# One product that turns and adds, shorter limits, hinted loops and a zeroing in blocks, in an attention and deformable-convolution kernel

## The chip, the cores and the metric

The kernel runs on one core of a Trainium2 chip, as one program. The core has a matrix engine (PE, which multiplies a weight tile held in it by a moving tile), and three engines for elementwise work: DVE (VectorE), ACT (ScalarE) and POOL (GpSimd). SP issues transfers. They run on their own and wait for each other on semaphores. The metric is the time of one execution in microseconds (us) on the device. Before the change the median of 3 runs was 2442.1 us (2438.3 to 2442.82).

## The reference

Two layers, cut to what matters. The change touches the second one alone.

```python
# layer 0: group norm, attention over 4096 positions of each of 4 images, x + projection
# layer 1, x: (4, 128, 64, 64) f32
out = relu(batchnorm(conv2d(x, w1), g1, b1))
offsets = conv2d(out, w_off) + b_off          # 18 channels: 9 row, 9 column offsets
out = batchnorm(deform_conv(out, offsets, w2), g2, b2)
return relu(out + x)
# deform_conv: per pixel and tap, p = pixel + tap + offset, limited to the padded image,
#   four neighbours gathered and weighted by distance, then a 3x3 product with w2
```

## The kernel before, in words

Each engine has its own instruction list, written by hand as a Python function under `@block`. A helper `after(engine, key, count)` makes the engine wait for a semaphore. Nothing is reordered: an engine runs its list as written. Where a list repeats, a loop with a register (`Fori`) runs on that engine alone, and the branch back at its end needs no other engine.

Four stages follow each other.

1. Attention (up to 1552 us in the trace), written by `schedule`. Its loops are not touched by the change.
2. The first 3x3 convolution (1567 to 1695 us), in 32 blocks of 512 pixels (8 image rows). POOL prepares the input (lines 412 to 421), ACT and DVE split it into two f16 parts, PE multiplies, and DVE writes `Y` and its statistics. Each engine has a loop over the 4 images.
3. The offset stage (1699 to 1828 us), again 32 blocks. For block n ACT makes `HT`, the normalised rows (line 608). DVE makes its two f16 parts `PDh` and `PDl` (lines 950 and 952), which PE needs one block later. PE turns `HT` by four transposes (line 1190) and multiplies the offset weights by 27 small products in four column groups of 32 (line 1200), so the sum over taps and parts ends up in four parts. Two blocks later PE turns these rows so that pixels stand on partitions (line 1208, four transposes per block). ACT copies them into `OR` (line 598), still as four parts. When all 8 blocks of an image are there, DVE runs `offset_finish` (lines 922 to 940): three additions of the parts, one of the bias, two limits and one maximum, each over 128x576 values. It stands in DVE's list after block 5 of the next image, and for the last image at the end. Beside this ACT and DVE stage the turned `HT` in one of two buffers `XS` (lines 583 and 957), and SP stores each block with four transfers (line 302). ACT must wait for those of two blocks earlier. POOL zeroes `Y` image by image once ACT has read it (line 435).
4. The sampling stage (1842 to 2391 us): 128 groups of 128 pixels, in 8 half images of 16 groups. POOL builds interpolation weights (line 457), PE transposes them (line 1227), ACT and DVE split them, PE samples and multiplies `w2`. PE runs the first half image outside a loop and the other seven in `pe.Fori(1, NHALF)` at line 1270, whose body is one half image: 960 products, each with a weight load. DVE's loop also has one half image a pass, those of ACT and POOL have two.

The numbers of a block run through all engines, so a late DVE block stops PE one block later, and through the copies of line 598 ACT too.

Of the kernel before, what the change touches and what calls it, by code (L numbers as in the profile page):

```python
# [28 lines left out]
NCH = N // 512  # L29
# [38 lines left out]
V_NW, V_NB, V_BQ, V_BK, V_BV, V_BP, V_G1, V_B1, V_G2, V_B2 = range(W_VEC, W_VEC + 10)  # L68
W_BOFF = W_VEC + 10
W_A = W_BOFF + NOFF  # L70
# [15 lines left out]
K_ALL = K_CB + 6  # L86
# [4 lines left out]
FIN = 7  # L91


def build(nc, x, weights, consts, out):
# [6 lines left out]
    with ctx:  # L101
# [60 lines left out]
        OR = sb_in(l1d, "offset_parts", [128, B * 32, 4, NOFF], F32)  # L162
# [75 lines left out]
        def vec(i):  # L238
            return WF[:, i:i + 1]

# [93 lines left out]
        def _(po):  # L334
# [88 lines left out]
            with po.Fori(0, B) as b:  # L423
                for rb in range(NCH):
                    conv1_in(b, rb)
# [36 lines left out]
            with po.Fori(0, npass) as n:  # L462
# [10 lines left out]
                with po.Fori(0, NHALF // 2 - 1) as u:  # L473
                    half_image(u * 2, 0, False)
                    half_image(u * 2 + 1, 1, False)
# [7 lines left out]
        def _(act):  # L483
# [88 lines left out]
            with act.Fori(1, B) as b:  # L572
                conv1_image(b, False)
# [43 lines left out]
            with act.Fori(1, B) as b:  # L617
                offset_image(b, range(NCH), False)
# [24 lines left out]
            with act.Fori(0, npass) as n:  # L643
# [28 lines left out]
                with act.Fori(0, NHALF // 2 - 1) as u:  # L672
# [13 lines left out]
        def _(ve):  # L686
# [14 lines left out]
            boff = WF[:, W_BOFF:W_BOFF + NOFF][:, None, :].to_broadcast([128, GPI, NOFF])  # L701
# [190 lines left out]
            with ve.Fori(1, B) as b:  # L892
# [29 lines left out]
            def offset_finish(b):  # L922
# [3 lines left out]
                parts = [OR[:, bass.ds(b * GPI, GPI), g, :] for g in range(4)]  # L926
                after(ve, "ocp", b * NCH + NCH)
                ve.tensor_tensor(od, parts[0], parts[1], ALU.add).then_inc(s["fin"], 1)
                after(ve, "fin", f0 + 1)
                ve.tensor_tensor(od, od, parts[2], ALU.add).then_inc(s["fin"], 1)  # L930
                after(ve, "fin", f0 + 2)
                ve.tensor_tensor(od, od, parts[3], ALU.add).then_inc(s["fin"], 1)
                after(ve, "fin", f0 + 3)
                ve.tensor_tensor(od, od, boff, ALU.add).then_inc(s["fin"], 1)
                after(ve, "fin", f0 + 4)
                ve.tensor_tensor(od, od, low, ALU.max).then_inc(s["fin"], 1)
                after(ve, "fin", f0 + 5)
                ve.tensor_tensor(od, od, HIGH[:, :, :], ALU.min).then_inc(s["fin"], 1)
                after(ve, "fin", f0 + 6)
                ve.tensor_reduce(SM[:, bass.ds(b + 48, 1)], od, AX.XY, ALU.max, apply_absolute_value=True).then_inc(s["fin"], 1)  # L940

            def h1_split(b, rbs, first):
                for rb in rbs:
# [18 lines left out]
            with ve.Fori(1, B) as b:  # L962
                h1_split(b, range(NCH), False)
            h1_split(B - 1, range(NCH, NCH + 2), False)
            offset_finish(B - 1)
# [6 lines left out]
            l1(ve.scalar_tensor_tensor(CNT[0:1, :], CL[0:1, K_CA - K_LO:K_CB - K_LO], SM[0:1, 30:31], CL[0:1, K_CB - K_LO:K_ALL - K_LO], ALU.mult, ALU.add))  # L972
            assert lstep[0] == L1_FLAG
            after(ve, "fz", B)
# [27 lines left out]
            with ve.Fori(0, npass) as n:  # L1002
# [25 lines left out]
                with ve.Fori(1, NHALF) as h:  # L1028
# [13 lines left out]
        def _(pe):  # L1042
# [122 lines left out]
            with pe.Fori(0, B) as b:  # L1165
# [15 lines left out]
            pe.wait_ge(s_wc, 4)  # L1181
# [184 lines left out]
```

## Time and profile before

| | us |
|---|---|
| median of 3 runs | 2442.1 |
| profiled execution, its own time | 2438.34 |
| its span, first to last instruction | 2436.4 |
| PE busy | 2260.8 |
| DVE busy | 1817.6 |
| ACT busy | 1797.5 |
| POOL busy | 1438.8 |

The profile is of one execution. Its time is 1.9 us more than its span, and it lies at the low end of the three runs. The granted clock (PEclk) is the share of full speed at which PE may run; its two levels are 1.2 and 2.4 GHz, so 0.50 means the lower one. Idle time is put down to what ended it; `issue` is idle time for which the profile shows no wait.

### The profile page before, as it was taken

What the parts mean: (1) busy time and instruction counts of PE and PEld (TensorE: products, weight loads), DVE (VectorE), ACT (ScalarE), POOL (GpSimd) and SP (SyncE); (2) the same over time, 40 slices, a digit from 0 to 9 for tenths busy, and PEclk for the clock granted to TensorE, in tenths of its full rate; (3) what the DMA queues carried; (4) which work ended last, traced back from release to release, by engine and by line L of the source; (5) the groups of instructions that cost most, each with busy time, mean ns of one, the idle gap of its engine ahead of it and who ended that gap; (6) DMA issues with size and microseconds to landing.
All of it is one profiled execution on the core that took longest, in us unless ns stands there. A gap on an engine that the chain in (4) does not pass through costs nothing.

```text
span 2436.4 us, 72880 instructions
## 1 busy us (share of the span) xinstructions
PE 2260.8 (93%) x26541; PEld 1819.8 (75%) x26541; DVE 1817.6 (75%) x3901; ACT 1797.5 (74%) x2963; POOL 1438.8 (59%) x1067
## 2 busy tenths in 40 slices
PE   5999999999999999999999999698867999999992
PEld 3777777777767777777777777587437999999992
DVE  6778877778877777877777777587666877777875
ACT  5788888888888888888888888432646766666764
POOL 4668656666656666655666666662117665556650
PEclk9999999999999999999999999899988999999996
DMA  3999999999999999998998999871224433333336
GB/s 92 194 174 169 171 180 166 177 176 173 177 176 161 174 177 173 172 160 155 177 175 176 175 177 176 222 226 49 74 66 140 123 116 116 115 116 115 115 100 276
DMA packets 1048676, 378.77 MB, mean 155 GB/s; under 512 B 975344, under 2 KB 1035376, under 8 KB 1040240
## 3 DMA queue, kind: packets, MB, share of 16 engines
q1 hardware_dynamic: 1048432, 375.42, 73.6%
q8 instruction: 165, 2.70, 0.5%
q14 instruction: 79, 0.65, 0.1%
HBM read 98.76 MB, written 41.68 MB: 58 GB/s over the span
## 4 chain that ended last, share of the span: by engine, by line
PE 70%; POOL 10%; issue 8%; DVE 4%; DMA 4%; ACT 1%; SPq 1%; POOLq 0%; DVEq 0%; ACTq 0%
PE psum L1045 14%; PE psum L1046 14%; PE psum L1047 14%; POOL probs_split L365 9%; PE psum L1085 7%; PE psum L1087 6%; PE psum L1086 6%; PE psum L1227 6%; DMA probsT_dma<-probs_split 2%; PE psum L1071 2%; PE psum L1200 1%; DMA final<-x_scratch 1%; DVE neg_max L714 1%; DVE padded_hi L950 1%; DMA xt_scratch<-xt_stage 0%
## 5 line engine op out<-in xcount | busy, mean ns | idle before, releaser
L365 POOL TENSOR_TENSOR probs_split<-probs,probs_split 128x896 f16<-128x896 f32 x512 | 967.2, 1889 | 526.6 <-ACT probs_split L515 526.5
L714 DVE TENSOR_REDUCE neg_max<-psum 128x1 f32<-128x1024 f32 x512 | 626.3, 1223 | 309.1 <-PE psum L1047 306.7
L512 ACT ACTIVATE probs<-psum,exp_bias 128x1024 f32<-128x1024 f32 x512 | 570.5, 1114 | 186.0 <-DVE exp_bias L716 184.8
L1085 PE MATMUL psum<-vT_hi,probsT_dma 128*128 128x129 f16 x3584 | 637.6, 221 | 12.9 <-DMA probsT_dma<-probs_split 12.7
L1087 PE MATMUL psum<-vT_hi,probsT_dma 128*128 128x129 f16 x3584 | 637.2, 219 | 0.0
L1086 PE MATMUL psum<-vT_lo,probsT_dma 128*128 128x128 f16 x3584 | 637.0, 218 | 0.0
L515 ACT ACTIVATE probs_split<-probs 128x896 f16<-128x896 f32 x512 | 486.5, 950 | 24.1 <-DMA probsT_dma<-probs_split 1.6
L457 POOL TENSOR_TENSOR interp<-row_hats,col_hats 128x360 f32<-128x360 f32 x384 | 294.8, 797 | 208.9 <-PE psum L1227 204.0
L1045 PE MATMUL psum<-k_hi,q_hi 128*128 128x512 f16 x1024 | 388.4, 379 | 4.0 <-DVE q_lo L830 2.5
L1046 PE MATMUL psum<-k_lo,q_hi 128*128 128x512 f16 x1024 | 388.6, 379 | 0.0
L1047 PE MATMUL psum<-k_hi,q_lo 128*128 128x512 f16 x1024 | 388.6, 379 | 0.0
L1085 PEld LDWEIGHTS psum<-vT_hi,probsT_dma 128*128 128x128 f16 x3584 | 347.5, 97 | 15.9 <-DMA probsT_dma<-probs_split 15.5
L1086 PEld LDWEIGHTS psum<-vT_lo,probsT_dma 128*128 128x128 f16 x3584 | 352.8, 98 | 0.0
L1087 PEld LDWEIGHTS psum<-vT_hi,probsT_dma 128*128 128x128 f16 x3584 | 345.0, 96 | 0.0
L984 DVE TENSOR_TENSOR interpT_lo<-psum,interpT_hi 120x384 f16<-120x384 f32 x384 | 191.1, 550 | 80.9 <-ACT interpT_hi L632 80.0
L641 ACT ACTIVATE sampled_hi<-psum 128x432 f16<-128x432 f32 (+1 forms) x384 | 182.6, 496 | 88.7 <-PE psum L1047 88.4
L992 DVE TENSOR_TENSOR sampled_lo<-psum,sampled_hi 128x432 f16<-128x432 f32 (+1 forms) x384 | 207.4, 554 | 49.7 <-ACT sampled_hi L641 45.4
L632 ACT ACTIVATE interpT_hi<-psum 120x384 f16<-120x384 f32 x384 | 162.0, 491 | 83.2 <-PE psum L1227 81.4
L1045 PE MATMUL psum<-sampled_hi,weights_hi 128*128 128x128 f16 x1152 | 215.3, 221 | 0.6 <-DVE sampled_lo L992 0.6
L1047 PE MATMUL psum<-sampled_hi,weights_lo 128*128 128x128 f16 x1152 | 213.9, 220 | 0.0
L1046 PE MATMUL psum<-sampled_lo,weights_hi 128*128 128x128 f16 x1152 | 213.6, 220 | 0.0
L1045 PE MATMUL psum<-interpT_hi,xt_windows 120*128 120x144 f16 x1024 | 211.0, 229 | 0.0
(181 smaller groups left out, 4898.2 us busy)
## 6 DMA issues: line engine op xcount, KB each, us to landing
xt_windows<-xt_scratch SPq DMA_DIRECT2D x192, 320.0 KB
xt_scratch<-zeros_f SPq DMA_DIRECT2D x28, 576.0 KB, 4.3
probsT_dma<-probs_split SPq DMA_TRANSPOSE x512, 4.0
x_residual<-x SPq DMA_DIRECT2D x128, 64.0 KB, 2.9
x_scratch<-x_out SPq DMA_DIRECT2D x128, 64.0 KB, 2.6
x_rows<-x_scratch SPq DMA_DIRECT2D x32, 256.0 KB, 3.4
xt_scratch<-xt_stage SPq DMA_DIRECT2D x128, 64.0 KB
final<-x_scratch SPq DMA_DIRECT2D x16, 512.0 KB, 10.2
```

What stands on the lines that cost most here:

```text
L365: po.tensor_tensor(PH[j][:, 1, :], P[:, j, 0:128 * DT[j]], PH[j][:, 0, :], ALU.subtract).then_inc(s["pl"], 1)
L457: last = po.tensor_tensor(SS[:, g % 2, :, WR * TW * a:WR * TW * a + WR * TW].rearrange("p k (j x) -> p k j x", j=WR), HX[:, hb, g, :, :, N ...
L512: act.activation(P[:, j, :], sc, ACT.Exp, bias=NB[:, par, j:j + 1]).then_inc(s["exp"], 1)
L515: act.activation(PH[j][:, 0, :], P[:, j, 0:128 * DT[j]], ACT.Copy).then_inc(s["ph"], 1)
L714: ve.tensor_reduce(NM[:, par, j:j + 1], sc, AX.X, ALU.max, negate=True).then_inc(s["mx"], 1)
L992: ve.tensor_tensor(lo, src, hi, ALU.subtract).then_inc(s["xl"], 1)
L1045: pe.matmul(dst, lh, rh, start=start, stop=False)
L1046: pe.matmul(dst, lh, rl, start=False, stop=False)
L1047: return pe.matmul(dst, ll, rh, start=False, stop=stop)
L1085: pe.matmul(dst, th, Vh[:, p, v, 0:129], start=n == 0, stop=False)
L1086: pe.matmul(dst[:, 0:128], th, Vl[:, p, v, :], start=False, stop=False)
L1087: last = pe.matmul(dst, tl, Vh[:, p, v, 0:129], start=False, stop=n == KT - 1)
```

## The change

- PE turns the offset rows by a matrix product and no longer by a transpose. The product's moving side is a 128x18 matrix of zeros and ones that adds the four column groups, so 18 columns per 128 pixels come out and not 128.
- The bias is added by ACT when it reads the rows from the accumulators (line 592 before).
- ACT copies 18 values a pixel straight into `OFF`; the tile `OR` goes.
- `offset_finish` has three steps (two limits and the maximum) and not seven, and one of them stands behind each of blocks 4, 5 and 6 of the next image.
- `Y` is zeroed in 32 pieces of 128x512 and not in 4 of 128x4096, each as soon as ACT has read it.
- Ten loops of PE, ACT, DVE and POOL in stages 2 to 4 are made by `repeat`, which puts a prefetch hint for the branch back at the head of each pass.
- PE waits once for the late constants, which hold the 0/1 matrix.

```diff
-FIN = 7
+FIN = 3
+        def repeat(eng, start, end):
+            return nc.Fori(start, end, engines=[eng.engine], hint_back_edge=True)
-            for b in range(B):
-                after(po, "hA", (b + 1) * NCH)
-                po.memset(Y[:, b, :], 0.0).then_inc(s["fz"], 1)
+            for m in range(B * NCH):
+                after(po, "hA", m + 1)
+                po.memset(Y[:, m // NCH, 512 * (m % NCH):512 * (m % NCH) + 512], 0.0).then_inc(s["fz"], 1)
-                    last = act.activation(dst, src, ACT.Copy)
+                    last = act.activation(dst, src, ACT.Identity, bias=vec(V_BO))
             def offset_pixels(m, par):
                 after(act, "ot", m + 1)
-                src = PS[:, 2 + par, :].rearrange("p (t g k) -> p t g k", t=4, g=4)[:, :, :, 0:NOFF]
-                act.activation(OR[:, bass.ds(m * 4, 4), :, :], src, ACT.Copy).then_inc(s["ocp"], 1)
+                src = PS[:, 2 + par, 0:4 * NOFF].rearrange("p (t k) -> p t k", t=4)
+                act.activation(OFF[:, bass.ds(m * 4, 4), :], src, ACT.Copy).then_inc(s["ocp"], 1)
-            def offset_finish(b):
+            def offset_finish(b, step):
...
-                ve.tensor_tensor(od, parts[0], parts[1], ALU.add).then_inc(s["fin"], 1)
-                ve.tensor_tensor(od, od, parts[2], ALU.add).then_inc(s["fin"], 1)
-                ve.tensor_tensor(od, od, parts[3], ALU.add).then_inc(s["fin"], 1)
-                ve.tensor_tensor(od, od, boff, ALU.add).then_inc(s["fin"], 1)
...
-                    if rb == 5 and not first:
-                        offset_finish(b - 1)
+                    if rb in (4, 5, 6) and not first:
+                        offset_finish(b - 1, rb - 4)
...
-                            last = pe.transpose(PS[:, 2 + rb % 2, tt], OE[:, rb % 2, tt], ident)
+                            last = pe.matmul(PS[:, 2 + rb % 2, NOFF * t:NOFF * t + NOFF], OE[:, rb % 2, tt], CL[:, K_SEL - K_LO:K_ALL - K_LO], start=True, stop=True)
...
-                with pe.Fori(1, NHALF) as h:
+                with repeat(pe, 1, NHALF) as h:
```

(The other nine loops change in the same way.)

On DVE, in the loop of the offset stage, this stands in a row before, from block 5 on. L950, L952 and L957 are one block's split and staging; L928 to L940 are `offset_finish`.

```order
L950 CAST padded_hi<-h_rows 128x8x64 [waits offset_conv,h1_ready]
L952 TENSOR_TENSOR padded_lo<-h_rows,padded_hi 128x8x64 [waits shift_steps]
L957 TENSOR_TENSOR xt_stage<-psum,xt_stage 128x4x128 [waits h1T_hi_ready]
L232 ISA
L928 ISA [waits offset_copied]
L928 ISA
L928 TENSOR_TENSOR offsets<-offset_parts 128x576
L232 ISA
L930 ISA [waits offset_steps]
L930 TENSOR_TENSOR offsets<-offsets,offset_parts 128x576
L232 REGISTER_ALU
L932 ISA [waits offset_steps]
```

Five more such steps follow before the next block's L950. This is DVE's list at the same place now, with the line numbers of the changed kernel (L946, L948 and L953 are the block's work, L929 and L932 the two limits).

```order
L953 TENSOR_TENSOR xt_stage<-psum,xt_stage 128x4x128 [waits h1T_hi_ready]
L231 ISA
L929 ISA [waits offset_copied]
L929 TENSOR_TENSOR offsets<-offsets,late_constants 128x576
L231 REGISTER_ALU
L946 CAST padded_hi<-h_rows 128x8x64 [waits offset_conv,h1_ready]
L948 TENSOR_TENSOR padded_lo<-h_rows,padded_hi 128x8x64 [waits shift_steps]
L953 TENSOR_TENSOR xt_stage<-psum,xt_stage 128x4x128 [waits h1T_hi_ready]
L231 ISA
L932 TENSOR_TENSOR offsets<-offsets,offset_high 128x576 [waits offset_steps]
```

One step now stands between two blocks, where seven stood. On PE, this is the head of the sampling loop now.

```order
L1268 UNCONDITIONAL_BRANCH
L1268 BRANCH_PREFETCH_HINT
L1268 ISA
L231 ISA [waits interp_ready]
L1225 MATMUL psum<-constants,interp 120x128 [waits interpT_lo_ready]
L1225 MATMUL psum<-constants,interp 120x128 x2
```

Before, the second of these rows was missing; the other instructions of the loop are the same.

## Rows read from the trace of the kernel before

**Rows 1.** The page, part 1: engine, busy us, share of span, instructions.
```profile
PE 2260.8 (93%) x26541; PEld 1819.8 (75%) x26541; DVE 1817.6 (75%) x3901; ACT 1797.5 (74%) x2963; POOL 1438.8 (59%) x1067
```

**Rows 2.** Waits of PE, whole run: total us, times, longest.
```profile
PE psum L1227 <- issue: 21.4, 6, 5.0
PE psum L1200 <- DVE padded_lo L952: 20.5, 5, 5.8
```

**Rows 3.** Timeline, PE, pass starts: start us, us, what, [idle before <- releaser].
```profile
1973.35 0.89 PE L1227 MATMUL psum<-constants,interp 128*120 128x128 f32 x3 [5.01 <-issue]
...
2041.97 1.32 PE L1227 MATMUL psum<-constants,interp 128*120 128x128 f32 x5 [2.87 <-issue]
...
2320.89 1.03 PE L1227 MATMUL psum<-constants,interp 128*120 128x128 f32 x5 [2.96 <-issue]
```

**Rows 4.** Timeline of POOL inside a pass: two groups in a row.
```profile
1961.40 2.30 POOL L457 TENSOR_TENSOR interp<-row_hats,col_hats 128x360 f32<-128x360 f32 x3 [1.70 <-PE psum L1227]
1965.40 2.30 POOL L457 TENSOR_TENSOR interp<-row_hats,col_hats 128x360 f32<-128x360 f32 x3 [1.70 <-PE psum L1227]
```

**Rows 5.** Windows at a pass boundary: busy us per engine, PEclk, DMA, GB/s.
```profile
1974.00:1976.00 2.00, 2.00 (x14) 1.94 (x13) 1.11 (x2) 1.43 (x3) 0.40 (x1) 0.50 0.00 0
1976.00:1978.00 2.00, 2.00 (x32) 2.00 (x31) 1.36 (x3) 0.87 (x3) 1.90 (x3) 0.88 0.04 8
1978.00:1980.00 2.00, 2.00 (x30) 1.99 (x27) 1.07 (x2) 1.15 (x4) 0.00 (x0) 1.00 0.22 37
```

**Rows 6.** Timeline of PE in the offset stage.
```profile
1711.77 0.64 PE L1190 MATMUL psum<-constants,h_rows 128*128 128x128 f32 x4
...
1714.48 0.64 PE L1190 MATMUL psum<-constants,h_rows 128*128 128x128 f32 x4
...
1749.65 0.61 PE L1200 MATMUL psum<-padded_hi,offset_w 128*32 128x512 f16 x2 [5.77 <-DVE padded_lo L952]
...
1816.10 0.64 PE L1190 MATMUL psum<-constants,h_rows 128*128 128x128 f32 x4
```

**Rows 7.** Timeline of PE weight loads in one block of that stage.
```profile
1713.98 0.42 PEld L1208 LDWEIGHTS psum<-constants,offset_rows 128*128 128x128 f32 x4 [0.43 <-issue]
1714.37 0.56 PEld L1190 LDWEIGHTS psum<-constants,h_rows 128*128 128x128 f32 x4
```

**Rows 8.** Weight loads of f32 products: L1129 by source, then by timeline.
```profile
L1129 PEld LDWEIGHTS psum<-small,constants x8: 186/189/333, 17.0 to 925.3; 128*128 128x128 f32 x8
...
925.17 0.30 PEld L1129 LDWEIGHTS psum<-small,constants 128*128 128x128 f32 x2 [0.82 <-DVE x_out L755]
...
6.92 0.50 PEld L1051 LDWEIGHTS psum<-weights_f 128*128 128x128 f32 x2 [6.92 <-POOLq L339]
7.30 0.55 PEld L1052 LDWEIGHTS psum<-weights_f 128*128 128x128 f32 x2
```

**Rows 9.** Timeline of DVE in the offset stage.
```profile
1718.54 3.82 DVE L950 CAST padded_hi<-h_rows 128x512 f16<-128x512 f32 x1 [0.95 <-ACT h_rows L608]
...
1741.03 0.75 DVE L928 TENSOR_TENSOR offsets<-offset_parts  x1
...
1746.13 0.75 DVE L940 TENSOR_REDUCE small<-offsets  x1 [0.15 <-DVE offsets L938]
1746.80 2.07 DVE L950 CAST padded_hi<-h_rows 128x512 f16<-128x512 f32 x1
...
1764.05 0.43 DVE L950 CAST padded_hi<-h_rows 128x512 f16<-128x512 f32 x1 [0.94 <-ACT h_rows L608]
...
1821.15 0.76 DVE L928 TENSOR_TENSOR offsets<-offset_parts 128x576 f32<-128x576 f32 x1 [2.46 <-ACT offset_parts L598]
```

**Rows 10.** Timeline of POOL there.
```profile
1718.56 3.51 POOL L435 MEMSET y_then_z<- 128x4096 f32 x1 [18.90 <-ACT h_rows L608]
```

**Rows 11.** Timeline of ACT there, one staging buffer.
```profile
1761.79 0.60 ACT L583 ACTIVATE xt_stage<-psum 128x512 f16<-128x512 f32 x1 [0.86 <-DMA xt_scratch<-xt_stage]
...
1767.47 0.60 ACT L583 ACTIVATE xt_stage<-psum 128x512 f16<-128x512 f32 x1 [0.82 <-DMA xt_scratch<-xt_stage]
```

More of the change, by code:

```diff
@@ L67 @@
 W_VEC = W_PROJ + C
-V_NW, V_NB, V_BQ, V_BK, V_BV, V_BP, V_G1, V_B1, V_G2, V_B2 = range(W_VEC, W_VEC + 10)
-W_BOFF = W_VEC + 10
-W_A = W_BOFF + NOFF
+V_NW, V_NB, V_BQ, V_BK, V_BV, V_BP, V_G1, V_B1, V_G2, V_B2, V_BO = range(W_VEC, W_VEC + 11)
+W_A = W_VEC + 11
 W_OFF = W_A
@@ L421, in conv1_in @@
                 po.tensor_tensor(VF[:, rb % 4, 3, :, :], ends[1][:, 1], ends[1][:, 0], ALU.subtract).then_inc(s["vf"], 1)
-            with po.Fori(0, B) as b:
+            with repeat(po, 0, B) as b:
                 for rb in range(NCH):
@@ L472, in _ @@
                     distances(n * NHALF, 0, 0, w)
-                with po.Fori(0, NHALF // 2 - 1) as u:
+                with repeat(po, 0, NHALF // 2 - 1) as u:
                     half_image(u * 2, 0, False)
@@ L571, in _ @@
             conv1_image(0, True)
-            with act.Fori(1, B) as b:
+            with repeat(act, 1, B) as b:
                 conv1_image(b, False)
@@ L616, in _ @@
             offset_image(0, range(NCH), True)
-            with act.Fori(1, B) as b:
+            with repeat(act, 1, B) as b:
                 offset_image(b, range(NCH), False)
@@ L671, in _ @@
                 half_image(0, 0, True, False)
-                with act.Fori(0, NHALF // 2 - 1) as u:
+                with repeat(act, 0, NHALF // 2 - 1) as u:
                     half_image(u * 2 + 1, 1, False, False)
@@ L891, in _ @@
             conv1_image(0, True)
-            with ve.Fori(1, B) as b:
+            with repeat(ve, 1, B) as b:
                 conv1_image(b, False)
@@ L920, in _ @@
             link(ve.tensor_scalar(HIGH[:, :, :], low, float(HH + 1), None, ALU.add))
-            def offset_finish(b):
+            def offset_finish(b, step):
                 f0 = b * FIN
                 od = OFF[:, bass.ds(b * GPI, GPI), :]
-                parts = [OR[:, bass.ds(b * GPI, GPI), g, :] for g in range(4)]
-                after(ve, "ocp", b * NCH + NCH)
-                ve.tensor_tensor(od, parts[0], parts[1], ALU.add).then_inc(s["fin"], 1)
-                after(ve, "fin", f0 + 1)
-                ve.tensor_tensor(od, od, parts[2], ALU.add).then_inc(s["fin"], 1)
-                after(ve, "fin", f0 + 2)
-                ve.tensor_tensor(od, od, parts[3], ALU.add).then_inc(s["fin"], 1)
-                after(ve, "fin", f0 + 3)
-                ve.tensor_tensor(od, od, boff, ALU.add).then_inc(s["fin"], 1)
[L935 to L940, printed above, removed]
+                if step == 0:
+                    after(ve, "ocp", b * NCH + NCH)
+                    ins = ve.tensor_tensor(od, od, low, ALU.max)
+                elif step == 1:
+                    after(ve, "fin", f0 + 1)
+                    ins = ve.tensor_tensor(od, od, HIGH[:, :, :], ALU.min)
+                else:
+                    after(ve, "fin", f0 + 2)
+                    ins = ve.tensor_reduce(SM[:, bass.ds(b + 48, 1)], od, AX.XY, ALU.max, apply_absolute_value=True)
+                ins.then_inc(s["fin"], 1)
             def h1_split(b, rbs, first):
@@ L957, in h1_split @@
                         ve.tensor_tensor(xs[:, :, C:2 * C], src, xs[:, :, 0:C], ALU.subtract).then_inc(s["xe"], 1)
-                    if rb == 5 and not first:
-                        offset_finish(b - 1)
+                    if rb in (4, 5, 6) and not first:
+                        offset_finish(b - 1, rb - 4)
             h1_split(0, range(NCH), True)
-            with ve.Fori(1, B) as b:
+            with repeat(ve, 1, B) as b:
                 h1_split(b, range(NCH), False)
             h1_split(B - 1, range(NCH, NCH + 2), False)
-            offset_finish(B - 1)
+            for step in range(FIN):
+                offset_finish(B - 1, step)
             after(ve, "fin", B * FIN)
@@ L1027, in _ @@
                 half_image(0, range(HALF), True)
-                with ve.Fori(1, NHALF) as h:
+                with repeat(ve, 1, NHALF) as h:
                     half_image(h, range(HALF), False)
@@ L1164, in _ @@
             after(pe, "wg", 14)
-            with pe.Fori(0, B) as b:
+            with repeat(pe, 0, B) as b:
                 for rb in range(NCH):
```

19 lines of the change are left out of this document (10 added, 9 removed).

## The prediction

> **What bounds the kernel now.** I read the page first. PE is busy 93% of the span, DVE, ACT and POOL 75%, 74% and 59% [rows 1], so I asked where PE stands still. The table of PE's waits answers: of the waits that this change can reach, two are large. Six waits of 21.4 us in all, the longest 5.0, stand before line 1227 and are put down to nothing ("issue"), and five of 20.5 us stand before line 1200 and end with DVE's line 952 [rows 2].
>
> The first six are in the sampling stage. The timeline of PE shows them where its loop of half images starts a pass: 5.01 us at 1973.35, 2.87 at 2041.97, 2.96 at 2320.89, with three more between [rows 3]. Seven passes have six branches back, and there are six waits. The change from the unlooped first half to the loop has none. The loops of the earlier stages on PE have none either, and their bodies are shorter: 288 products a pass in the first convolution and 280 in the offset stage, against 960. So I read the wait as the fetch of the loop's first instructions, which were pushed out by a body longer than the store. Inside a pass a group takes 4.00 us (POOL's line 457 repeats from 1961.40 to 1965.40) [rows 4], so a half image is worth 64.0 us. From 1973.35 to 2320.89 are five passes in 347.5 us [rows 3]. Five at 64.0 make 320.0, their five waits 16.4 (21.4 less the first 5.0), and 11.1 are left, 2.2 a pass. The windows show what these are: after the wait the granted clock is 0.50 in one window and 0.88 in the next, then 1.00 [rows 5]. That is 1.0 and 0.24 us lost in these two windows, and about 0.3 in the 0.65 us between the start at 1973.35 and the first of them, 1.6 in all. PE ran at the upper level until it stood idle, and came back on the lower one.
>
> The other five waits are in the offset stage. A block of it takes PE 2.71 us undisturbed (line 1190 at 1711.77 and at 1714.48). From 1711.77 to 1816.10, however, 28 blocks take 104.3 us, and 28 x 2.71 are 75.9 [rows 6]. So 28.4 us are stalls and their after-effects. The timeline of DVE names two causes. The seven steps of `offset_finish` stand in a row from 1741.03 to 1746.13 plus 0.75, about 5.9 us at 0.79 each, and the cast of the next block comes behind them. That cast itself takes 2.07 us, another 3.82, where an ordinary one takes 0.43 [rows 9]. The long ones lie beside POOL's zeroing of an image, 3.51 us at 1718.56 [rows 10]. PE then waits 5.77 us at 1749.65 [rows 6].
>
> **The change, part by part.**
>
> Hints. The one that counts is PE's in the sampling loop. If the target is there in time, the 21.4 us go. The slow clock behind them goes too, since nothing but these waits makes PE idle there; of the 2.2 us a pass I take the 1.6 that the windows behind a wait explain, six times, 9.6 us. Together 31.0. The bounds are 0 and 21.4 + 6 x 2.2 = 34.6. In the other nine loops PE shows no such wait, so nothing is there to gain, and one more instruction a pass on an engine with idle time costs nothing; without that cover I would bound it by one short step, 0.2 us for each of some 20 passes, 4 us. What is late next at a pass's start is DVE, the busiest engine beside PE; at 75% of the span [rows 1] it has room for a step back of its own.
>
> The zeroing. Four pieces of 3.51 us become 32 of about 0.44 (3.51 / 8), each released by the same event as DVE's cast of that block. Now and then such a cast waited a whole piece (3.82 against 3.51 + 0.3). So I take 0.4 us more for each cast. It lies in idle time: at 1764.05 DVE had stood idle 0.94 us before its cast [rows 9]. At the start of the stage there is no such room, since PE waits for the first casts; I take 0.6 us there. If the cast wins each race the price is nothing, and if the room is gone it is 32 x 0.4 = 13 us.
>
> The Trainium skill (SBUF — State Buffer, section "Who interferes with whom") says that a cast in a two-port mode and a POOL instruction exclude each other, and that whoever issues first has the pair of ports for the whole instruction. The 3.82 us agree; by this rule a cast that comes first pays nothing, so the sum would be the same or 0.6 us better.
>
> `offset_finish`. Seven steps in a row become three, each alone between two blocks. One is 0.76 us, 0.79 with its gap. What hides it is DVE's idle time: 0.94 us in a block of 2.84 [rows 9, 11], and 0.36 more when the block grows to 3.2 (next paragraph), 1.3 in all, against 0.8 for a step and 0.4 for the zeroing. So I cost them at nothing in the loop; without that cover, 12 steps of 0.8 would cost 10 us. With the short zeroing this removes all 28.4 us. At the end of the stage nothing hides them: from 1821.15 on the seven are on the path to the flag, and four fewer save 4 x 0.79 = 3.2 us.
>
> The turning. Now four transposes take one weight load each; from the first of them to the first of line 1190 are 0.39 us (1713.98 to 1714.37) [rows 7]. The trace has no 18-column product in f32, but it has f32 products that are no transposes. These are recorded with two weight loads per product: line 1129 has 8 for four calls, 186 to 189 ns each at full clock, and two of them take 0.30 us together, so 0.11 apart. At the lower clock two (line 1051) run from 6.92 and the next pair from 7.30, 0.19 each, which is 0.095 at full clock [rows 8]. So eight loads take between 8 x 0.095 = 0.76 us and, if none overlaps the one before, 8 x 0.187 = 1.5 us. I take 8 x 0.11 = 0.9, by the row at full clock. PE's block grows by 0.5 us to 3.2 (bounds 0.37 and 1.1), and PE stays the bound there: the store buffers come round in 5.68 us for two blocks (1761.79 to 1767.47) [rows 11], 2.84 each. 28 blocks cost 14.0 us, block 2 another 0.5, and three such products behind the last line 1190 1.2 (the last one waited for ACT anyway).
>
> On the count of passes the Trainium skill (FP8 and Floating Point Precision, section "FP22 (1s8e13m) — PE Internal Precision") has true f32 go through the array in four. The trace shows two pairs of records per product and 0.11 us from one to the next. By four at that distance the block would grow by 16 x 0.11 - 0.39 = 1.4 us and not 0.5 (rival B).
>
> ACT. Adding the bias in a pass that is made anyway costs nothing, and copying 72 values a block and not 288 can only shorten an instruction, for which I count nothing. PE's wait for the late constants is met, since DVE's line 920 reads them before the stage's first block.
>
> **The sum.** Offset stage: -28.4 + 14.0 + 0.5 + 0.6 + 1.2 - 3.2 = -15.3. Sampling: -31.0. Together -46.3 us. From the profiled execution's 2438.3 (its span 2436.4 and 1.9 around it) this is 2392.0; from the median of the runs, 3.8 higher, 2395.8. I say 2393.
>
> **The rivals.**
>
> A, the hint does nothing on PE. Its mark is passed 960 products before the branch; if the engine forgets it or can't hold the target while it runs on, the six waits stay. Then the gain is 15.3 us: 2426.8 from the median. For it speaks that the trace shows no hint at work anywhere. The Trainium skill (Runtime: NRT & Kernel Launch, section "Instruction fetch mechanics") calls the prefetch purely sequential and says that a taken branch to a target out of the window stalls for a fetch; by that rule the time is this rival's. The first half agrees with the six waits; whether a hint breaks it no row can say. Chance 0.15. A partial effect (half of the waits) would end near 2411, 0.05.
>
> B, the product is dear. If each of eight loads takes its full 0.187 us, the block grows by 1.1, which over 32 blocks is 19 us more than I took, and the offset stage gains nothing: 2393 + 19 = 2412. Against it speaks that the loads at 925.17 overlap [rows 8]. Chance 0.07. If a product takes sixteen loads at 0.11 us, the block grows by 1.4: 32 x 0.9 = 29 us more, 2422. Against it speak the 8 records for 4 calls. Chance 0.03. This is the skill's count of four passes.
>
> C, slower. The eight passes run one behind the other, each load and then a product at least as long, 0.37 us or more a pass. That is 3.0 us a block for 0.39, and 32 x 2.6 = 83 us against the 62 that the other parts save (28.4 + 3.2 + 31.0 - 0.6): 2442 + 21 = 2463. It decides from 1.9 us more a block, 0.29 us a pass; the rows at 0.11 speak against it. Chance 0.04.
>
> D, the change does most of what it says but the short zeroings and steps leave some 6 to 8 us of stalls: 2400, inside the range; I count it with the forecast, which has 0.66 in all.
>
> **Numbers.** The forecast's own range is 2384 to 2404. Below it, 2380 needs the low price of the product and all of the clock. Up to 2428 the range takes in A and B. A difference under 0.2% (4.9 us) can't be told from none here. Faster 0.93 (forecast, A, B), within 0.2% 0.03, slower 0.04.
>
> **What would show it.** PE's waits before the first transposes of a pass are gone, and the granted clock stays at 1.00 across them. Right for the turning are eight weight loads a block in 0.9 us and 3.2 us from block to block. No wait of more than 1 us for DVE is left in the offset stage, no cast is over 0.9 us, and that stage is 15 us shorter. I am wrong if the six waits stay, if the block is over 3.5 us, or if DVE's cast still holds PE.

## The result, and the profile after

The change makes the kernel faster, by about half of what was forecast.

| | before (4 runs) | after (4 runs) | forecast |
|---|---|---|---|
| median, us | 2440.2 | 2416.15 (2415.32 to 2419.25) | 2393 |
| after / before | 1 | 0.9905 [0.9889, 0.992] | 0.981 |
| span of the profiled run | 2436.4 | 2413.5 | 2390 |
| first `HT` transposes to first interpolation | 140.7 | 126.2 | 125.4 |
| sampling, first interpolation to the start of the last nine products of `w2` | 548.4 | 539.2 | 517.4 |

The 2442.1 us ahead of the prediction is the median of three of the four runs before; the fourth took 2437.66.

The offset stage came out as worked out (-14.5 us, forecast -15.3). Sampling gained 9.2 us and not 31.0. Ahead of the offset stage 0.3 us are gained, and behind sampling 1.1 us are lost again, which makes the 22.9 us between the spans.

The page after, part 1, against [rows 1]. Busy times hardly moved: the change acts on waits.

```profile
PE 2262.6 (94%) x26669; PEld 1827.2 (76%) x26669; DVE 1806.1 (75%) x3885; ACT 1798.3 (75%) x2963; POOL 1438.8 (60%) x1095
```

There are 128 more matmuls and loads: one extra pair of records for each of the 128 turning products. PE's waits after, which answer [rows 2]:

```profile
PE psum L1225 <- issue: 15.1, 6, 4.0
PE psum L1198 <- DVE padded_lo L948: 3.2, 2, 1.7
```

The wait for DVE fell from 20.5 us to 3.2. The six waits at the passes' starts are still six, 15.1 us for 21.4. The timeline of PE shows them, against [rows 3]:

```profile
1956.07 1.22 PE L1225 MATMUL psum<-constants,interp 128*120 128x128 f32 x9 [2.14 <-issue]
2023.73 1.20 PE L1225 MATMUL psum<-constants,interp 128*120 128x128 f32 x9 [1.76 <-issue]
...
2295.30 2.17 PE L1225 MATMUL psum<-constants,interp 128*120 128x128 f32 x9 [4.01 <-issue]
```

The windows behind the first of them, against [rows 5]. The lower clock level is still granted after four of the six waits; the last row is the one behind the wait of 1.76 us, where the clock stays at 1.00, as it does after the 1.83 us at 2157.68.

```profile
1956.00:1958.00 2.00, 1.93 (x17) 1.93 (x18) 0.76 (x2) 1.26 (x3) 0.63 (x1) 0.77 0.04 8
1958.00:1960.00 2.00, 2.00 (x21) 2.00 (x19) 1.54 (x4) 0.53 (x1) 1.67 (x3) 0.50 0.00 0
1960.00:1962.00 2.00, 2.00 (x31) 2.00 (x29) 0.73 (x2) 0.94 (x2) 0.00 (x0) 0.87 0.00 0
...
2024.00:2026.00 2.00, 2.00 (x30) 1.99 (x29) 1.09 (x3) 1.61 (x4) 0.99 (x2) 1.00 0.05 12
```

The offset stage, weight loads of PE in a block, against [rows 7]:

```profile
1715.17 0.97 PEld L1206 LDWEIGHTS psum<-late_constants,offset_rows 128*128 128x128 f32 x8 [0.43 <-issue]
1715.98 0.62 PEld L1188 LDWEIGHTS psum<-constants,h_rows 128*128 128x128 f32 x4
...
1718.36 0.97 PEld L1206 LDWEIGHTS psum<-late_constants,offset_rows 128*128 128x128 f32 x8 [0.43 <-issue]
```

Eight loads take 0.81 us up to the next line (1715.17 to 1715.98), 0.10 apart, and the block is 3.19 us (1715.17 to 1718.36). DVE there, against [rows 9], one step behind each block and the casts between them:

```profile
1738.63 0.75 DVE L929 TENSOR_TENSOR offsets<-offsets,late_constants 128x576 f32 x1
1739.74 0.83 DVE L946 CAST padded_hi<-h_rows 128x512 f16<-128x512 f32 x1 [0.36 <-ACT h_rows L610]
...
1741.82 0.75 DVE L932 TENSOR_TENSOR offsets<-offsets,offset_high 128x576 f32 x1
1745.32 0.83 DVE L946 CAST padded_hi<-h_rows 128x512 f16<-128x512 f32 x1 [2.76 <-ACT h_rows L610]
```

The groups of the casts and of POOL's zeroing ([rows 10] before), min/median/max in ns:

```profile
L946 DVE CAST padded_hi<-h_rows x32: 424/746/837, 1700.9 to 1798.7; 128x512 f16<-128x512 f32 x32
```

```profile
L437 POOL MEMSET y_then_z<- x32: 524/524/565, 1700.9 to 1798.7; 128x512 f32 x32
```

The cast is held in 30 of 32 blocks (746 ns in the median for 424), and in the loop DVE still stands idle for ACT before most of the next ones, so it costs nothing there. The rule of the Trainium skill (SBUF — State Buffer, section "Who interferes with whom") that the two exclude each other agrees: a cast begun beside the zeroing ends 0.28 us after it. Its order rule does not show in the recorded starts: in 12 blocks the cast is recorded 0.02 to 0.03 us ahead of the zeroing and takes 0.83 us all the same, as at 1745.32. The end of the stage and the way to sampling:

```profile
1812.08 0.37 PE L1215 MATMUL psum<-constants,small 128*1 128x128 f32 x1 [2.89 <-DVE small L964]
...
1827.30 2.95 PE L1225 MATMUL psum<-constants,interp 128*120 128x128 f32 x11 [14.85 <-POOL interp L459]
```

### The profile page after: what moved, and what is told of

It is laid out like the page before. It is cut to its first block, busy times and chain, and to the rows that moved or that the text cites. A ratio compares the mean times of both kernels' runs of the same rounds, so it can differ in the third digit from the quotient of the medians.

```text
span 2413.5 us, 73170 instructions
## 1 busy us (share of the span) xinstructions
PE 2262.6 (94%) x26669; PEld 1827.2 (76%) x26669; DVE 1806.1 (75%) x3885; ACT 1798.3 (75%) x2963; POOL 1438.8 (60%) x1095
## 3 DMA queue, kind: packets, MB, share of 16 engines
q1 hardware_dynamic: 1048432, 375.42, 66.7%
## 4 chain that ended last, share of the span: by engine, by line
PE 74%; POOL 11%; issue 7%; DVE 3%; DMA 3%; ACT 1%; SPq 0%; POOLq 0%; ACTq 0%; DVEq 0%
PE psum L1042 14%; PE psum L1043 14%; PE psum L1044 14%; POOL probs_split L367 9%; PE psum L1082 7%; PE psum L1084 7%; PE psum L1083 7%; PE psum L1225 5%; PE psum L1198 2%; DMA probsT_dma<-probs_split 2%; PE psum L1068 2%; PE psum L1206 1%; PE psum L1188 1%; DMA final<-x_scratch 1%; DVE neg_max L715 1%
## 5 line engine op out<-in xcount | busy, mean ns | idle before, releaser
L1082 PEld LDWEIGHTS psum<-vT_hi,probsT_dma 128*128 128x128 f16 x3584 | 347.5, 97 | 13.5 <-DMA probsT_dma<-probs_split 13.4
```

The lines of the kernel that those rows point to most:

```text
L1082: pe.matmul(dst, th, Vh[:, p, v, 0:129], start=n == 0, stop=False)
```

## The experiments

Each ratio is to the kernel before on the same chip, with its 95% interval. "Sampling" is the stretch of the table above. Line numbers are each kernel's own. In the traces queue q8 carries instructions in packets of 16 KB (59 are 0.97 MB). I take them for PE's, since they stop when PE's loop needs no fetch (below). A sampling time is that of the one execution whose trace was kept.

**Hint off on PE's sampling loop (nohint).** Does the hint do anything?

```diff
-                with repeat(pe, 1, NHALF) as h:
+                with nc.Fori(1, NHALF, engines=[pe.engine]) as h:
```

> The changed kernel with the hint of PE's sampling loop taken out, the other nine hints kept. Fetch-position theory (the hint lets the fetch of the loop's first block start when the list enters the block that holds the branch back, which in the changed layout is only about 1 us before the branch): the six waits grow from 15.1 us to about 21 us, some 1 us each, and the time from 2416 to about 2424. Rival, the hint does nothing and the difference 21.4 to 15.1 is scatter: the waits stay near 15 us, the time near 2416. Also told apart here: if the slow pass starts come from the other engines' hints, they would go.

2436.26 us, 0.998 [0.9967, 0.9993]; sampling 557.8 us. PE's waits:

```profile
PE psum L1225 <- issue: 28.7, 6, 6.0
```

Both expectations missed. The hint is worth 18.6 us of sampling (557.8 - 539.2), twice what the result suggested, and the waits without it are longer than before the change (28.7 for 21.4) on a loop of the same instructions. Something else in the change makes sampling 9.4 us longer (557.8 - 548.4). The medians say the same without the traces: `nohint` is 5.3 us below the kernel before (2436.26 to 2441.57), though the offset stage gains 14.5.

**The hint alone on the kernel before (bhint).**

```diff
-                with pe.Fori(1, NHALF) as h:
+                with nc.Fori(1, NHALF, engines=[pe.engine], hint_back_edge=True) as h:
```

> The kernel before with nothing but the hint on PE's sampling loop. In its layout the fetch behind the last block starts 5.6 us before the last product, not 1.1 as in the changed kernel. Fetch-position theory: with that lead the hinted block is there in time, the six waits (21.4 us) fall to below 3 us in all, and the time falls by about 30 us, to about 2410. Rival, a hint takes 1 us off each wait wherever it stands: waits of about 15 us stay and the time is about 2431.

2423.49 us, 0.9925 [0.9903, 0.9946], a gain of 18 us. This lies between the two expectations. The waits before L1227 are gone and a smaller one stands before the 30th product of each pass (7.6 us in six; the seventh, 2.09 us, is at the loop's exit):

```profile
PE psum L1047 <- issue: 9.7, 7, 2.8
```

So the size of the hint's effect was wrong even without the rest of the change: 18 and not 31.

**The loop's head moved (slot0, slot100).** Same instructions, but the loop begins at slot 0 or 100 of a fetch block.

```diff
+                with nc.Fori(1, NHALF, engines=[pe.engine], hint_back_edge=True, head_slot={pe.engine: 0}) as h:
```

> The changed kernel with the head of PE's sampling loop placed at the start of a fetch block (slot 0 of 256). The body of about 2040 instructions then ends near slot 249 of its eighth block, so the hinted fetch can start almost a whole block (8 us) before the branch. Fetch-position theory: all six waits before the first transposes of a pass are gone, the granted clock stays at 1.00 there, the sampling stage is 22 to 25 us shorter, the time about 2392. Rival, a hinted branch back out of a long body costs a fixed 2 to 4 us: waits of about 15 us in all stay, time near 2416.

2401.2 us, 0.9835 [0.9812, 0.9858], sampling 523.5 us. That is 15.7 us less and not the 22 to 25 expected. No pass starts with a wait any more. What is left stands at the loop's entry and exit:

```profile
1895.70 1.19 PE L1225 MATMUL psum<-constants,interp 128*120 128x128 f32 x9 [1.38 <-issue]
...
2348.90 0.30 PE L1042 MATMUL psum<-interpT_hi,xt_windows 120*128 120x144 f16 x1 [2.48 <-issue]
```

And q8 goes quiet once the first pass has run (its last packet is at 1944.2). From 1897 to 2346, queue, packets, MB, share, first here and then in the changed kernel:

```profile
q8 instruction: 6, 0.10, 0.1%
```

```profile
q8 instruction: 59, 0.97, 0.9%
```

> The changed kernel with the head of PE's sampling loop at slot 100 of a fetch block, hinted. The branch back then stands near slot 93 of the ninth block, so the hinted fetch starts about 2.9 us before it. Fetch-position theory: waits at pass starts between those of slot 0 (none) and of the changed kernel (15.1 us in six): under 5 us in all, with one fetch a block, nine a pass. Rival, only a body that fits the store (slot 0) helps: six waits of about 15 us.

One run, 2402.1 us; sampling 525.2. The waits sum to 5.7 us, a little over the 5 expected. Three of the six waits are 0.55, 2.09 and 2.13 us, though q8 fetches all through the loop (61 packets):

```profile
PE psum L1225 <- issue: 5.7, 6, 2.1
```

Placement alone thus moves the hinted kernel by 14 to 16 us.

**Slot 0 without the hint (slot0_nohint).** Is it the placement or both?

> The changed kernel with the head of PE's sampling loop at slot 0 and no hint on it. The run with slot 0 and the hint made no fetch at all between 1896 and 2346 us, as if eight blocks stayed in the store. If the block behind the branch is fetched anyway without the hint and pushes the first one out, six waits of about 3 us each are back, with fetches all through each pass: time 2420 or more. Rival, the placement alone did it: no waits and about 2401.

One run, 2433.1 us; sampling 556.2. The waits are back, and so are the packets (57 from 1897 to 2346):

```profile
PE psum L1225 <- issue: 24.2, 7, 5.1
```

So at slot 0 the hint is worth 32.7 us (556.2 - 523.5), in the layout of the change 18.6, while without a hint slot 0 brings next to nothing (557.8 to 556.2).

**Where the 9.4 us come from (nohint_all, nohint_slot188, before_slot40).** The changed kernel with no hint anywhere; `nohint` with its loop at slot 188, where I estimate that it lay before the change; and the kernel before with its loop at slot 40, where the change has it.

```diff
-                with pe.Fori(1, NHALF) as h:
+                with nc.Fori(1, NHALF, engines=[pe.engine], head_slot={pe.engine: 40}) as h:
```

> The changed kernel with no hint on any of its ten loops. Open is why the changed kernel without PE's hint in sampling (nohint) takes 557.8 us there, 9.4 more than the kernel before (548.4), though that loop holds the same instructions. Theory: the loop lies elsewhere in the fetch blocks, because more instructions stand ahead of it; the hints of the other nine loops do nothing, so this kernel is like nohint, 555 to 560 us of sampling and about 2436 us. Rival: the hints on the loops of ACT, DVE and POOL disturb PE's fetches, and without them sampling is back at 548 and the time at 2427.

> nohint with the head of PE's sampling loop at slot 188 of a fetch block of 256. From the packets of the kernel before I estimate that its branch lies 5.6 us deep in its block; at 8 us a block that is slot 180, and a body of some 2040 instructions (960 products with a load each and 120 others) puts the head at about 188. Theory (placement makes the 9.4 us): sampling falls from 557.8 to about 548 to 551, the waits before L1225 from 28.7 to 21 to 24. Rival (something else in the change): 556 to 558 as in nohint.

> The kernel before with the head of PE's sampling loop moved to slot 40, where by the same estimate the changed kernel has it (branch 1 us deep in its block), no hint. Theory: sampling grows from 548.4 to about 557, the waits before L1227 from 21.4 to about 28, and the time from 2442 to about 2451, so ratio 1.004. Rival (not the placement): 548 and ratio 1.000.

`nohint_all`, one run: 2430.4 us, sampling 555.9, waits 28.2: like `nohint`, so the other engines' hints are not the cause (the time came out 6 us lower than expected; sampling is 2 us of it). `nohint_slot188`, one run: 2426.3 us, sampling 550.1. `before_slot40`: 2451.85 us, 1.005 [1.0032, 1.0068], sampling 561.4. PE's waits in these two:

```profile
PE psum L1225 <- issue: 19.7, 6, 4.9
```

```profile
PE psum L1227 <- issue: 31.7, 6, 7.0
```

The longer waits go away with the old place and come with the new one, on either kernel. It is the placement. The slots 188 and 40 are estimates. That the first is near the truth shows in one more row: `nohint_slot188` stands still for 0.73 us before the 30th product of its first pass, the product before which `bhint` waits in the place that the loop had before.

**A body of half the length (short, short_plain).** PE's loop runs 8 groups a pass and not 16, fifteen passes and not seven. `short` keeps the hints, `short_plain` has none in all ten loops. The renamed function's body is left out here.

```diff
-                half_image(0, range(HALF), True)
-                with repeat(pe, 1, NHALF) as h:
-                    half_image(h, range(HALF), False)
+                quarter_image(0, range(HALF // 2), True)
+                with repeat(pe, 1, 2 * NHALF) as h:
+                    quarter_image(h, range(HALF // 2), False)
```

> The changed kernel with a body of 8 groups (480 products, about 1020 instructions) in PE's sampling loop and twice the passes: 15 passes, 14 branches back. If the waits come from a body longer than the instruction store, no pass start waits, no fetch stands beside them, and the time is about 2392. Rival, each branch back costs the wait that is seen now (2.5 us and as much slow clock as goes with it): 8 more of them, time about 2440.

> As the run with the body of 8 groups, and the hint taken out of all ten loops. If a body that fits the instruction store needs no hint, and the other nine hints have no effect, pass starts stay without waits and the time stays at 2390, within 3 us. Rival, the hints are what keeps the short passes fed: waits before line 1225 come back and the time is over 2400.

2390.15 us, 0.979 [0.9773, 0.9806], and 2390.25 us, 0.9783 [0.9756, 0.9809]. Neither has an "issue" wait on PE at all. In `short` sampling is 516.0 us and the granted clock does not fall (window: us, busy of PE, PEld, DVE, ACT, POOL, then PEclk):

```profile
1825.60:2341.60 516.00, 514.12 (x7653) 510.92 (x7653) 429.67 (x926) 376.31 (x796) 331.62 (x395) 1.00 0.40 119
```

From 1880 to 2338 the view of the queues lists no q8 at all:

```profile
q1 hardware_dynamic: 8164, 53.45, 39.3%
q14 instruction: 9, 0.07, 0.1%
```

This is the whole 31 us that the forecast gave to the hints (548.4 - 516.0 = 32.4). PE's own hint has no part in it: its loop waits for no instruction with it or without. The two medians are equal, but the traces are not. In `short_plain` sampling takes 520.2 us, and PE waits twice, 2.7 us in all, for DVE, which waits for ACT. From one group to the one 16 later, where PE needs 64.1 us in every pass of `short`, two passes of `short_plain` take 66.6 and 66.7. They begin with groups 48 and 80 (counted from 0), where ACT's own sampling loop goes back. What this costs the other three runs of `short_plain` (2387.3 to 2395.6 us) no trace shows.

**The same on the kernel before (before_short).** The edit of `short` with a plain loop, and nothing of the change.

> The kernel before with only the body of PE's sampling loop cut to eight groups (15 passes, no hint); nothing of the change is in it. Theory: no wait at a pass's start and none of the slow clock behind it. From first interpolation to last sampled product 548.4 us become about 517, so the time falls by 31 us to about 2410 and this one edit is worth more than the whole change (24). The offset stage stays at 125.5 us. Rival: the placement of the loop makes some waits stay, as it did with the hint alone (2423), and the time is 2416 to 2424.

2411.16 us, 0.9866 [0.9847, 0.9884]; the offset stage is as before (125.9 us from the first transposes to the flag's product). This one edit gains 33 us by the medians, the whole change 24. Sampling is 521.8 us, 26.6 less than before and not the 31 expected. PE has no "issue" wait, but the two waits behind ACT's loop stand out here as well, and the passes that they begin take 67.0 and 68.6 us and not 64.1:

```profile
PE psum L1227 <- DVE interpT_lo L984: 3.9, 2, 2.2
```

```profile
2035.76 1.26 ACT L632 ACTIVATE interpT_hi<-psum 120x384 f16<-120x384 f32 x3 [4.68 <-issue]
```

PE made the first transposes of this group at 2030.97, and ACT takes them 4.8 us later, where 0.6 is usual. It stands still there for 4.2 to 5.1 us in all four kernels whose ACT loop has no hint and whose PE starts its passes on time (`bhint`, `before_short`, `short_plain`, `best`; in some the trace puts it down to a PE product and not to "issue"). It does not in those with ACT's loop hinted and PE on time (`slot0`, `short`, `turn_back`, `zero4`, `fin5`). So ACT's hint does something: without it two passes lose 5.1 to 7.4 us together in the three kernels with the short body. In the kernel before, PE's own waits at the same two places cover this.

**The turning undone (turn_back, best).** On `short`: four transposes, `OR` and six steps of `offset_finish` again, in twos and ones behind blocks 4 to 7, the bias left in ACT. `best` is the same without hints.

```diff
...
-  last = pe.matmul(PS[:, 2 + rb % 2, NOFF * t:NOFF * t + NOFF], OE[:, rb % 2, tt], CL[:, K_SEL - K_LO:K_ALL - K_LO], start=True, stop=True)
+  last = pe.transpose(PS[:, 2 + rb % 2, tt], OE[:, rb % 2, tt], ident)
...
-                    if rb in (4, 5, 6) and not first:
-                        offset_finish(b - 1, rb - 4)
+                    if 4 <= rb < NCH and not first:
+                        for step in ((0, 1), (2, 3), (4,), (5,))[rb - 4]:
+                            offset_finish(b - 1, step)
```

> The short-body kernel with the transposes and the tile OR put back in place of the 18-column product. The bias stays in ACT. Six steps (three additions, two limits, the maximum) stand as 2, 2, 1 and 1 behind blocks 4 to 7. By the price of the product as measured (block 3.19 us against 2.71) PE's block falls back, the store buffers then bound it at 2.84: 28 x 0.35 = 10 us less, less 1 at the end; against it 3 more steps at the end (2.4 us) and two blocks per image with two steps, 1 us each of stall, 5 to 6 in all: 2385 to 2388. Rival, the double steps cost as much as they did before: 2390 or more.

2390.12 us, 0.9783 [0.9754, 0.9812], the rival's time. From the first transposes to the flag's product are 106.3 us, 4.4 less than in `short` (110.7). But the loop's exit now waits, and the total is the same:

```profile
2337.75 0.23 PE L1047 MATMUL psum<-sampled_hi,weights_hi 128*128 128x128 f16 x1 [2.70 <-issue]
```

> The kernel of turn_back (eight-group sampling body on PE; transposes, OR and six finish steps in the offset stage) with no hint on any of the ten loops. Theory: the hint makes PE fetch the loop head and pushes out the block behind the branch, so turn_back paid 2.70 us at the loop's exit and got nothing for it; without hints that wait goes, the body still fits, and the 4.4 us that the offset stage gained stay: about 2385 us, 5 less than short and short_plain. Rival: the exit must be fetched anyway (it has not run before), so the wait stays and the time is turn_back's, 2390.

2387.08 us, 0.9761 [0.9747, 0.9776], the lowest median, though its interval still touches those of `short` and `turn_back`. The exit is free of that wait, and what is left there is 0.56 us for DVE:

```profile
2340.05 0.23 PE L1047 MATMUL psum<-sampled_hi,weights_hi 128*128 128x128 f16 x1 [0.56 <-DVE sampled_lo L994]
```

That wait is not all that the hints change: sampling is 520.4 us here and 518.8 in `turn_back`, because ACT's loop stands still twice (PE's passes of 66.6 and 67.0 us). A kernel like `best` with the hint on ACT's loop alone was not run. Its offset stage runs 28 blocks in 83.1 us, 2.97 each (2.71 to 3.37), and PE's loads show the transposes' 0.39 us again:

```profile
1751.22 0.42 PEld L1211 LDWEIGHTS psum<-constants,offset_rows 128*128 128x128 f32 x4 [0.43 <-issue]
1751.61 0.56 PEld L1193 LDWEIGHTS psum<-constants,h_rows 128*128 128x128 f32 x4
...
1754.24 0.42 PEld L1211 LDWEIGHTS psum<-constants,offset_rows 128*128 128x128 f32 x4 [0.43 <-issue]
```

So the product of 18 columns is a loss against this arrangement of the steps: 3.19 us a block for 2.97, and 110.7 us to the flag for 104.9.

**Which part took the stalls away (zero4, fin5).** Each is `short` with one part turned back: `Y` zeroed in four pieces, or the three steps in a row behind block 5.

```diff
-                po.memset(Y[:, m // NCH, 512 * (m % NCH):512 * (m % NCH) + 512], 0.0).then_inc(s["fz"], 1)
+                po.memset(Y[:, b, :], 0.0).then_inc(s["fz"], 1)
```

> The short-body kernel with Y zeroed in 4 pieces again. Theory: each piece holds one cast of DVE for 3.5 us, with PE's room of about 1 us that is 2 to 3 us of stall for each of four, the offset stage 8 to 10 us longer, time about 2399. Rival, the pieces did no harm and all of the 28.4 us of stalls came from the seven steps: the stage unchanged or 1 us shorter (no cast is slowed in the other 28 blocks).

```diff
-                    if rb in (4, 5, 6) and not first:
-                        offset_finish(b - 1, rb - 4)
+                    if rb == 5 and not first:
+                        for step in range(FIN):
+                            offset_finish(b - 1, step)
```

> The short-body kernel with the three steps in a row behind block 5, not one behind each of blocks 4, 5 and 6. Theory: 2.4 us in a row against 1.1 us of DVE's idle time and 1 us of PE's room: 0.5 to 1.5 us of stall for each of three images, the stage 2 to 4 us longer. Rival, spreading them is worth as much as shortening them: over 8 us.

One run each. `zero4`: 2400.3 us, 121.0 us to the flag, 10.3 more than `short`, with five waits for DVE:

```profile
PE psum L1198 <- DVE padded_lo L948: 9.0, 5, 2.1
```

`fin5`: 2390.45 us, 111.7 us to the flag, 1.0 more, which is less than the 2 to 4 expected and can't be told from none: kernels with the offset stage of the change take 110.3 to 111.9. So with three steps left, the short zeroing is what counts and spreading them is not. What the cut from seven steps to three brings alone no run separates: `best` has six steps, spread over four blocks, and waits 2.1 us for DVE in the stage, where the kernel before waits 20.5.

## Why the prediction was half right

**The step that failed** is "Hints. The one that counts is PE's in the sampling loop. If the target is there in time, the 21.4 us go ... Together 31.0." It gave the hint 31.0 us, and sampling gained 9.2. The diagnosis held: the wait is the fetch of a body that the store can't hold. `short`, `slot0` and the q8 lines show it. The price of all six waits and their clock (31.0, at most 34.6) held too: 32.4 measured in `short`, where ACT's loop is hinted, and 26.6 in `before_short`, where it is not. The cure was mis-sized, for two reasons.

- *The hint is no switch.* I gave it all or nothing (rival A), with 0.05 for half. In the change's layout it brings 18.6 us, alone on the kernel before 18, at slot 0 it brings 32.7. The packets suggest how. Around one branch back they are:

```
            end of pass | packets of q8, us              | first product of the next
before      ~2107.5     | 2101.9, 2107.5, 2110.8, 2114.2 | 2110.29
after       ~2088.0     | 2079.3, 2086.9, 2090.3         | 2089.93
```

  Inside a pass the packets come about 8 us apart. Before, one arrives at the branch itself and the pass starts 3 us after it. After, it comes at 2086.9, 1 us ahead of the branch, and the pass again starts 3 us after it. My reading is that the hint lets PE fetch the target when it enters the block that holds the branch; the gain is the lead from there, and here the branch stands near the head of its block. That the place decides is shown (slot 0 and 100 with the hint, 40 and 188 without); this rule for it is argued from the times.

- *A cost that stood nowhere in the sum.* `nohint` is slower than before in sampling by 9.4 us, on a loop body of the same instructions. It lies elsewhere. My reading is that the turning products (two pairs of records each), the hints and the wait for the constants put more instructions ahead of it; no run separates them. I counted the product's time and not its length in the instruction stream. The forecast of 31.0 less 9.4, and less the 12.4 by which the hint fell short (31.0 - 18.6), is the 9.2 measured; the terms come from the same traces, so this is bookkeeping and no check. `nohint_slot188` takes 7.7 of the 9.4 away and `before_slot40` puts 13.0 on the kernel before, by the placement alone. Why the waits vary from pass to pass within a kernel (1.8 to 4.0 us) stays open.

A second sentence did not hold, though it moved the forecast little: "In the other nine loops PE shows no such wait, so nothing is there to gain". It looked for ACT's waits in PE's rows, where PE's own covered them. Without ACT's hint 5.1 to 7.4 us are lost once PE is on time. It also has a price, which the prediction put at nothing and bounded at 4 us: ACT stands still once in the offset stage (next list) and once for 2.3 to 3.5 us behind the exit of its sampling loop, in all ten kernels with the hint and in none of the seven without.

The Trainium skill (Runtime: NRT & Kernel Launch, section "Instruction fetch mechanics") gave rival A its rule, that a taken branch out of the window stalls for a fetch. `nohint` (28.7 us of waits) agrees, `slot0` (none from pass to pass) shows that a hint can lift it. The window that the section gives, two pages, does not fit PE: `short` goes back without a wait over 480 products and their loads.

The Trainium skill (FP8 and Floating Point Precision) has the four passes of rival B in its section "TensorE Precision Notes", not in the one that the prediction names. The trace has two pairs of records a product, and the block grew by 0.48 us (3.19 - 2.71), not by that rival's 1.4.

**The steps that held.**

- Turning: eight loads in 0.9 us forecast, 0.81 measured; block 3.2, measured 3.19. Rivals B and C fall by that. The row of two overlapping loads in [rows 8] was the right one to go by.
- Stalls: from block 3 to block 31 are 90.8 us (PE's first transposes at 1712.89 and 1803.73). 28 x 3.19 are 89.3, so 1.5 us of stalls are left of 28.4. No cast is over 0.84 us. Behind the first block one wait for DVE of more than 1 us remains, 1.44 us at 1746.94, and "no wait of more than 1 us" was one of my marks. It is not DVE's doing: ACT stands still for 2.33 us before, with nothing to wait for:

```profile
1744.48 0.81 ACT L610 ACTIVATE h_rows<-y_then_z,small 128x512 f32 x1 [2.33 <-issue]
```

  This is the 15th of ACT's 32 blocks and not the start of a pass (its passes begin with the 9th, 17th and 25th). It comes with the hints: `nohint` shows it (2.12 us), `nohint_all` does not, and of the others all with a hint on ACT's loop have it (1.5 to 2.4 us) and none without. Why it stands in the middle of a pass is open.

  The start of the stage costs 1.5 us (1.1 forecast). The seven steps in the loop are 0.85 us apart and not 0.79, since two of them wait 0.15 us; nothing hangs on it.
- The end: from the last transposes to the flag's product 10.8 us became 8.35, -2.5 for the -2.0 of the sum (1.2 - 3.2). So -26.9, +13.4, +1.5 and -2.5 make the -14.5. The forecast was 0.8 us off; its four errors (1.5, -0.6, 0.4 and -0.5) partly cancel, which is luck.
- What I did not ask: whether the turning was worth its price. I charged it 14.0 us and never set against that a kernel that keeps the transposes. `best` does: it has 104.9 us to the flag where `short` has 110.7 and the kernel before 125.5.

Rival A's own time (2426.8) was 10.7 us above the result. It left out the 18.6 us that the hint does bring and the 9.4 us that the displaced loop costs. The partial effect that I put at 2411, with 0.05, was the nearest.

## What to carry to other kernels

A wait at the head of each pass that the trace puts down to nothing is a question to the instruction queue: count its packets inside the loop, and if the body doesn't fit, shorten the body before you hint the branch (33 us here, against 18 for the hint). Then ask the same of the other engines' loops in their own rows, since the longest wait hides theirs. With a body too long, the place of the loop moves the time (8 to 13 us here without a hint), so count an edit's instructions and not only its microseconds. When a part of a change costs 14 us and is carried by others that save 28, price it against leaving it out.

## What the hardware showed that I had not expected

- PE's store held a body of 960 products, each with its load, once the head lay at slot 0 and the branch was hinted: 6 packets in 449 us against 59. Without the hint, 57.
- A hint can cost something at the loop's exit. On PE there are waits of 2.09 (`bhint`), 2.48 (`slot0`) and 2.70 us (`turn_back`), none in the other five kernels with PE's hint (the changed one among them) and none in those without. On ACT there is one of 2.3 to 3.5 us in all ten with its hint. I read it as the block behind the branch giving way to the target; no run tests that.
- A wait at a pass's start can cost more than itself, since the granted clock falls from 1.00 to 0.50 behind it. Beside the waits themselves, a pass lost 1.8 us before ((548.4 - 21.4 - 516.0) / 6) and 2.2 in `nohint`. The length of the wait does not decide alone: in `bhint` the clock stays at 1.00 after 2.84 us at 2239.35 and falls to 0.61 and 0.54 in the 2 us windows after 2.84 us at 2306.42.
- A product of 18 columns in f32 leaves two pairs of records, 0.10 us apart.
